# A decoder layer on one core: the first cross-attention is prepared in the last steps of self-attention, and the down projection's weights are split later

## What is computed

```python
x = x + attn(layernorm(x))          # 16 heads of 128, q and k RMS-normalised, no mask
x = x + xattn(layernorm(x), ctx)    # 16 heads of 32, causal mask, keys and values from ctx (361 x 128)
x = x + ffn(layernorm(x))           # silu(gate) * up, 1408 wide, then down; two of 8 experts
                                    # add low-rank terms of rank 16 to gate, up and down
```

## Time and profile before

| | |
|---|---|
| median of 3 runs | 2619.14 us (2618.99 to 2619.47) |
| the profiled execution | 2618.98 us, its span 2617.2 us |
| PE busy | 2477.4 us, 95% |
| DVE, ACT, POOL busy | 1545.2, 1343.3, 866.8 us |
| chain that ended last | PE 82%, DVE 7%, ACT 4%, issue 3% |
| granted clock of PE, mean | 0.979 |

### The profile page before, as it was taken

How to read it: one execution, slowest core, us unless ns; L and a number is a source line. 1 busy time by engine, 2 the same in 40 slices (tenths; PEclk the granted TensorE clock), 3 DMA queues, 4 the chain that set the end, 5 groups by cost and what they waited for, 6 DMA issues and landing times.

```text
span 2617.2 us, 47837 instructions
## 1 busy us (share of the span) xinstructions
PE 2477.4 (95%) x16390; PEld 1334.0 (51%) x16390; DVE 1545.2 (59%) x3589; ACT 1343.3 (51%) x4098; POOL 866.8 (33%) x801
## 2 busy tenths in 40 slices
PE   6999999999999999999769999999999999999998
PEld 3455455555554555445344464464464465465466
DVE  7777756666666666667355555554645645645634
ACT  4555555555555555555354454454554554454433
POOL 3333333333333333324123323323323322423412
PEclk9999999999999999999869999999999999999999
DMA  5677777776777668797320001001001001000000
GB/s 154 156 176 167 155 159 153 172 170 145 157 171 157 155 154 186 168 187 166 107 77 10 16 2 37 16 2 37 15 4 37 7 12 37 1 17 24 7 17 8
DMA packets 455401, 235.37 MB, mean 90 GB/s; under 512 B 389096, under 2 KB 391784, under 8 KB 455144
## 3 DMA queue, kind: packets, MB, share of 16 engines
q1 hardware_dynamic: 455144, 232.08, 38.3%
HBM read 78.66 MB, written 32.77 MB: 43 GB/s over the span
## 4 chain that ended last, share of the span: by engine, by line
PE 82%; DVE 7%; ACT 4%; issue 3%; POOL 1%; DMA 1%; SPq 1%; DVEq 0%; POOLq 0%; ACTq 0%
PE ps L1380 22%; PE ps L1381 21%; PE ps L1382 21%; PE ps L1513 3%; PE ps L1514 2%; PE ps L1515 2%; ACT mem L887 2%; PE ps L1624 2%; PE ps L1523 1%; PE ps L1527 1%; PE ps L1525 1%; PE ps L1566 1%; PE ps L1612 1%; PE ps L1586 1%; PE ps L1554 1%
## 5 line engine op out<-in xcount | busy, mean ns | idle before, releaser
L1380 PE MATMUL ps<-mem 128*128 128x512 f16 (+6 forms) x3924 | 1204.4, 326 | 59.5 <-issue 24.6
L1381 PE MATMUL ps<-mem 128*128 128x512 f16 (+6 forms) x3924 | 1217.5, 325 | 0.0
L1382 PE MATMUL ps<-mem 128*128 128x512 f16 (+6 forms) x3924 | 1201.1, 325 | 0.0
L1380 PEld LDWEIGHTS ps<-mem 128*128 128x128 f16 (+3 forms) x3924 | 407.6, 104 | 380.8 <-issue 75.8
L1382 PEld LDWEIGHTS ps<-mem 128*128 128x128 f16 (+3 forms) x3924 | 408.7, 104 | 311.7 <-issue 9.3
L1381 PEld LDWEIGHTS ps<-mem 128*128 128x128 f16 (+3 forms) x3924 | 410.4, 105 | 300.3 <-issue 9.6
L699 POOL TENSOR_TENSOR mem<-mem 128x500 f32<-128x500 f32 (+1 forms) x231 | 268.1, 1160 | 360.2 <-ACT mem L949 207.5
L649 POOL TENSOR_TENSOR mem<-mem 128x8 f32<-128x8 f32 x100 | 163.7, 1637 | 518.3 <-DVE mem L1021 518.3
L795 ACT ACTIVATE mem<-ps,mem 100x100 f32<-100x100 f32 x512 | 169.2, 345 | 223.4 <-DVE mem L1051 222.3
L1336 DVE TENSOR_TENSOR mem<-mem 128x500 f16<-128x500 f32 (+1 forms) x231 | 144.5, 649 | 188.7 <-ACT mem L931 184.7
L661 POOL TENSOR_TENSOR mem<-mem 100x400 f16<-100x400 f32 x128 | 158.4, 1237 | 175.7 <-ACT mem L805 175.7
(11 more groups left out here) (121 smaller groups left out, 3132.5 us busy)
## 6 DMA issues: line engine op xcount, KB each, us to landing
x<-mem SPq DMA_DIRECT2D x100, 256.0 KB, 2.9
mem<-x SPq DMA_DIRECT2D x75, 256.0 KB, 3.5
mem<-in_x SPq DMA_DIRECT2D x50, 256.0 KB, 3.6
mem<-x SPq DMA_DIRECT2D x12, 1000.0 KB
mem<-mem SPq DMA_DIRECT2D x32, 200.0 KB
out<-mem SPq DMA_DIRECT2D x6, 1000.0 KB
mem<-in_wq SPq DMA_DIRECT2D x16, 256.0 KB, 4.0
mem<-in_wk SPq DMA_DIRECT2D x16, 256.0 KB, 4.2
```

What stands on the lines that cost most here:

```text
L1380: pe.matmul(out_ap, ah, bh, start=(i == 0), stop=False)
L1381: pe.matmul(out_ap, ah, bl, start=False, stop=False)
L1382: mm = pe.matmul(out_ap, al, bh, start=False, stop=(i == len(pairs) - 1))
```

## The change

The preparation of the first cross-attention is taken out of `cross_attention` and put into the last four steps of self-attention by a function `begin_cross(n)` on PE, ACT and DVE:

- step 126 (`B_KEYS`): row tiles 0 and 1 are turned, keys 0 to 2;
- step 127 (`B_TURN`): key 3, row tiles 2 and 3;
- step 128 (`B_VALUES`): five value products;
- step 129 (`B_QUERIES`): four query products.

On PE this stands in a step ahead of the mix and the output projection; on ACT and DVE it is the last of a step. The wait for the last add (`s["add"], ALL`) in front of the first turn is gone. So that this is free of overlaps in memory, `yT` lies over weights that are used up, and qkT, vt and others move within the buffer.

The pieces of `bd` and `wd` are no longer among `B_PIECES` (16 are left). Piece 13, 14 and 15 are split in batches 0, 1 and 2 of the first cross-attention, one each. The others are loaded into the buffer `yn` once it is free, and are split in chunks 1, 3 and 5 of the feed-forward part of group 0 (`load_late`, `late_hi`, `late_lo`); the layer norm of the next group moves from chunks 6 and 7 to 8 and 9 there. For that, group 0 is written out, and the loop has four passes, groups 1 to 4. In the diff, the first `begin_cross` is DVE's, the second PE's; ACT's takes the same rows, values and queries as they come.

```diff
+        B_KEYS, B_TURN, B_VALUES, B_QUERIES = STEPS - 2, STEPS - 1, STEPS, STEPS + 1
...
         def over_groups(eng, group):
-            with eng.Fori(0, FULL - 1) as g:
+            group(0, GB, GB)
+            with eng.Fori(1, FULL - 1) as g:
                 group(g, GB, GB)
...
-        LN_STATS_CHUNK, LN_ROWS_CHUNK = FC - 5, FC - 4
+        def ln_chunks(g):
+            return (FC - 3, FC - 2) if isinstance(g, int) and g == 0 else (FC - 5, FC - 4)
...
-        add_pieces(bd_hi, bd_lo, bd, 1, E)
-        add_pieces(wd_hi, wd_lo, wd, FC, E)
-        assert len(B_PIECES) == 20
+        assert len(B_PIECES) == 16
+        LATE_AT = {1: 0, 3: 1, 5: 2}
+        late = yn.rearrange("p t e -> p (t e)")
...
         def beside_first(b):
-            return range(len(B_PIECES))[B_IN_A + 2 * b:B_IN_A + 2 * b + 2]
+            return range(len(B_PIECES))[B_IN_A + b:B_IN_A + b + 1]
...
                     sp.wait_ge(c["moved"], g + 1)
                     sp.wait_ge(c["yn"], g * 2 * NT + 2 * nt)
+                    if isinstance(g, int) and g == 0:
+                        for k in range(3):
+                            load_late(k)
+                        sp.wait_ge(c["latelo"], 3)
                     load_rows(yn, ahead, nxt, "yn_in")
...
+                def late_hi(k):
+                    act.wait_ge(c["late"], 16 * (k + 1 + (k == 2)))
+                    for hi, stage, _ in late_parts(k, True):
+                        op = act.activation(hi, stage, ACT.Copy, scale=W_SCALE)
+                    op.then_inc(c["latehi"], 1)
...
+            def begin_cross(n):
+                if n == B_KEYS:
+                    for t in range(2):
+                        row_lo(0, t, TM, t)
+                    for m in range(3):
+                        take_ck(0, GS, m)
+                if n == B_TURN:
+                    take_ck(0, GS, 3)
+                    for t in range(2, NT):
+                        row_lo(0, t, TM, t % 2)
...
+            def begin_cross(n):
+                if n == B_KEYS:
+                    pe.wait_ge(c["mask"], 5)
+                    pe.wait_ge(s["klo"], ALL)
+                    for t in range(2):
+                        turn_row(0, yn, t, TM, t)
+                    pe.wait_ge(c["wkv"], 16)
+                    pe.wait_ge(c["ctx"], 16)
+                    pe.wait_ge(s["vlo"], ALL)
+                    for m in range(3):
+                        keys(0, GS, m)
+                if n == B_TURN:
+                    pe.wait_ge(s["exp"], STEPS)
+                    keys(0, GS, 3)
+                    for t in range(2, NT):
+                        pe.wait_ge(c["lnlo"], t - 1)
+                        turn_row(0, yn, t, TM, t % 2)
+                if n == B_VALUES:
+                    for b in range(GB):
+                        cross_values(0, b)
+                if n == B_QUERIES:
+                    pe.wait_ge(c["lnlo"], NT)
+                    pe.wait_ge(c["wlo"], B_FIRST)
+                    for m in range(KC):
+                        queries(0, GS, m)
...
                 for u in projected_at(n):
                     project_qk(u)
+                begin_cross(n)
                 if 0 <= n - 1 < STEPS:
                     mix_values(n - 1)
                 for w in summed_at(n):
                     project_wo(w)
-            pe.wait_ge(s["add"], ALL)
-            pe.wait_ge(c["wlo"], B_FIRST)
-            pe.wait_ge(c["wkv"], 16)
-            pe.wait_ge(c["mask"], 5)
```

More of the change, by code:

```diff
@@ L277, in decoder_layer @@
                  "rl top rexp chain spread mT mTe a am ahi alo base gb sg0 ub lora gs us sgs "
-                 "h hhi hlo ad dt dsum dhi dlo yp add moved")
+                 "h hhi hlo ad dt dsum dhi dlo yp add moved late latehi latelo")
         c = {n: sem("c_" + n) for n in names.split()}
@@ L1330, in layer, with late_lo @@
                                       ALU.subtract).then_inc(c["alo"], 1)
+                def late_lo(k):
+                    dve.wait_ge(c["latehi"], k + 1)
+                    for lo, stage, hi in late_parts(k, False):
+                        op = dve.scalar_tensor_tensor(out=lo, in0=stage, scalar=W_SCALE, in1=hi,
+                                                      op0=ALU.mult, op1=ALU.subtract)
+                    op.then_inc(c["latelo"], 1)
                 def lo_h(i, j):
@@ L1500, in wide, with keys, cross_values @@
                                        yT_hi[:, e, 0:gs], yT_lo[:, e, 0:gs]) for e in range(KC)])
+            def keys(g, gs, m):
+                pe.matmul(ps[:, 2 + m, 0:gs], cwkv[:, m * P:(m + 1) * P], ctxT[:, 0:gs],
+                          start=True, stop=True).then_inc(c["ck"], 1)
+            def cross_values(g, b):
+                if b < 2:
+                    pe.wait_ge(c["cke"], g * KC + b + 1)
+                else:
+                    pe.wait_ge(c["ve"], g * GB + b - 1)
+                pe.matmul(ps[0:S, 2 + b % 2, :], ctxT[:, b * S:(b + 1) * S], cwkv[:, E:2 * E],
+                          start=True, stop=True).then_inc(c["v"], 1)
@@ new lines, in _ @@
+            for n in range(FIRST_STEP, STEPS + 2):
+                if 0 <= n + 1 < STEPS:
+                    scores(n + 1)
+                for u in valued_at(n):
+                    project_v(u)
+                for u in turned_tile(n):
+                    turn_rows(u)
+                for u in projected_at(n):
+                    project_qk(u)
+                begin_cross(n)
+                if 0 <= n - 1 < STEPS:
+                    mix_values(n - 1)
+                for w in summed_at(n):
+                    project_wo(w)
```

174 lines of the change are left out of this document (102 added, 72 removed).

## The result

The changed kernel takes 2602.83 us as the median of 5 runs (2597.96 to 2604.31), against 2619.47 of the kernel before in the same session (2618.99 to 2625.26). The ratio is 0.9929, interval 0.9917 to 0.994. It is worked out over all runs and is not the quotient of the two medians, which is 0.9936. On the 2619.14 of the prediction the ratio gives 2600.5, where 2605.2 was forecast and 2601.0 was the low end. The change gains more than I gave it. Built and timed again it gave 2604.27 against 2620.82, ratio 0.9934 (0.992 to 0.9947). One execution of the kernel with only group 0 unrolled took 6607 us, in a slow state, and stands in none of the figures.

What follows compares the result with a forecast made beforehand. PE bounds the feed-forward part; the self-attention tail and first cross-attention hold waits. Gains 6.7 + 5.9 + 0 + 1.2 = 13.8 us, taken from 2618.98, give 2605.2 us, range 2601 to 2611.5.

Steps and rivals of the forecast that it cites:

- part 4: Loop over groups: with group 0 outside, one of four DVE issue stalls goes, gaining 1.2 us (bounds 0 to 2.5).
- Part 1: Self-attention steps 126 to 129: cross-attention preparation fills PE idle time, first mask at about 1288.2 against 1294.88, gaining 6.7 us.
- rival D: Steps 127 and 128: two gaps keep the clock low through the moved work, slower at 2625.6 us; chance 0.04.
- C: Step 127: DVE's queue gives the filled gap back, mask stays at 1294.9, price 6.7 us, total 2611.9; chance 0.06.
- Part 2: First cross-attention: five weight pieces leave for later or go one per batch, gaining 5.9 us.
- rival A: First cross-attention: split gain comes only by half through low-clock scores or late DMA, 3 us less, 2608 to 2611; chance 0.12.
- Part 3: Feed-forward part of group 0: three late weight pieces are hidden in ACT and DVE idle time, costing 0 us.
- B: Feed-forward of group 0: late pieces not hidden, PE waits up to 2.3 us in three chunks, 2612 us; chance 0.08.

## Why the prediction fell short

The forecast was 13.8 us less. The two ratios give 18.6 and 17.3, the medians 16.6 in both sessions, the first profiles 16.3. Three steps of the sum failed. It took everything ahead of step 127 as unchanged and gave it no width in the range; the first profiles differ by 2.97 there. It took the rest of group 0 at 0; group 0 lost 2.45. It took part 4 at 1.2; the unrolling brought 2.55 to 2.9. For the first of these no reason was given; for the second it was that PE has no idle time there, which says nothing of its clock.

**Part 1, the preparation: right.** 6.7 was worked out, 6.5 came in the first pair of profiles, and the preparation alone gives 6.6; against the mean of the four old tails it is 7.2. The step through step 127 was right in detail: a wait of about 3 and one of about 2 (3.16 and 2.01), and the mix, forecast at 1263.1, at 1259.85; with 2.97 added for the earlier start of the step that is 1262.8. The clock was 1.00 from 1268 to 1288, so rival D was out, and the mask came early, so C was.

**Part 2, one piece per batch: right, a little small.** The mixes of the five batches stand 14.35, 23.99, 33.79, 43.01 and 54.94 us behind the mask; before they stood 15.84, 26.24, 39.29, 49.18 and 61.37. So the batches gained 1.49, 0.76, 3.25, 0.67 and 0.26, where the prediction had 1.3, then 4.1 for two, and 0.5. The gain of the split did not come by half (rival A), and the DMA came in time: the load is issued at 1286.69, and ACT begins the piece straight behind its exponentials:

```profile
1292.87 1.48 ACT L795 ACTIVATE mem<-mem 128x1408 f16<-128x1408 f32 x1
```

**Part 3, late pieces in group 0: the mechanism right, the figure for the group wrong.** The late pieces cost 0 as predicted, and B is out. The failed step is that the rest of group 0 was taken to be as it was ("PE has no idle time there"). The group took 2.45 more, because in these profiles the clock is low for longer at its router (+1.55) and again in the next cross-attention (+1.26). I had looked for the clock's answer in the tail alone, though the earlier trace rows show 0.66 in the very stretch whose rhythm the change alters. What makes it low at 137 us behind the router, with PE busy 5.90 of 6 us there and no edit near, no run settles; that one kernel of seven escapes both, with the same program up to there as another that does not, says that the edit alone does not decide it.

**Part 4, group 0 outside the loop: too small.** 1.2 was the stall in one pass. The kernel with this alone gained 2.9 in groups 0 to 4, and groups 1 to 4 of the kernel after 2.55. The term was mis-sized in its basis: it counted PE's wait behind one stall, which came as 0.9 (router to spread in group 1, 7.50 before and 6.59 after). Group 0, written out, also takes 0.25 less in the chunks, and with nothing but the unrolling 0.36 less between mask and router; the three stalls that are left are 2.28 to 2.40 instead of 2.51 to 2.54, and router to spread is 0.14 to 0.26 shorter behind them. Another 0.8 of the 2.55 is the clock's again: in group 2 spread to chunk 1 took 19.10 before, with 0.72 in the 6 us from 8 us behind the router, and takes 18.29 after, at 1.00. My upper bound of 2.5 was a little below what came.

**The sum and the range.** Terms 3 and 4 nearly cancel in the profile after (+2.45 and -2.55, where 0 and -1.2 stood). What made the profiled time 16.3 shorter instead of 13.8 is the start-up and self-attention before step 127, -2.97, for which I had nothing, neither in the sum nor in the range, and by which two executions of one kernel differ. The ratios put the kernels 17.3 and 18.6 us apart (0.9934 and 0.9929), the medians 16.6 in both sessions, and the stages from step 127 on give 13.3 between the first two profiles and 16.5 between the second pair (1371.18 and 1354.72), 14.9 in the mean; part of what the first pair lacks is the old tail, short in that profile. The 1.7 to 3.7 us that remain are not placed by any one profile; by the sum of the stages they would lie before step 127. In the eight other kernels the same remainder, the ratio's gain less that of the stages from step 127 on (against the mean of the two profiles of before), lies between -3.0 and +4.7, so it is of the size of the scatter. Whether the other layout of the buffer makes self-attention shorter on average stays open: it took 1206.7 in the mean of the three profiles with the old layout and 1205.6 in that of the nine with the new one, a difference far inside the scatter. That the time fell below the low end is thus in part luck, and what failed is also the range: its low end had the bounds of the terms, and neither the scatter of the stages ahead of the change nor that of the old tail.

## What to carry over

Work moved into waits of the bounding engine pays what it fills less the waits that it makes, and that can be worked out from the queue of the engine that takes the results; the largest thing left was the weight piece and the key copies standing in that queue ahead of what PE needed, and moving them took another 7.7 us from the tail. After a change of rhythm in a stretch with a low clock, expect the times at low clock to move and to be worth one to three us elsewhere, check the stages downstream even though no instruction of theirs changed, and take a second profile before a cause is given: here two executions of the same code differed by 2.3 and by 3.0 us in neighbouring stages. Before a range is drawn, know how far the long stages that are not touched differ between executions: here 3 us in each pair and 8.6 over twelve.

## What the runs showed of the hardware

- The granted clock of a stretch is not a property of the work in it. Group 0 took 200.3 to 200.4 us in six of the seven profiles with one piece per batch of the first cross-attention, 197.3 in the seventh, and 197.3 to 198.3 in the five with another distribution. The difference is 0.64 instead of 0.84 behind the router, and 0.72 instead of 1.00 in 6 us that begin 137 us later, where PE was busy 5.90 of them. The same program up to there gave 200.31 in one execution and 197.33 in another.
- A loop pass that follows a jump costs 1.4 us more than the same pass written out (198.91 against 197.53, 198.76 against 197.31). Of that, 0.7 to 1.0 stands near the start of the pass, where DVE shows 2.3 to 2.4 us of "issue" some tiny instructions in. The first pass, with no jump before it and no stall, still costs 0.9 more (198.43 against 197.52).
- A POOL product that reads SBUF and a DVE operation with two SBUF inputs hold each other back: DVE's low half took 1.21 instead of 0.68 us when the product had started first, and the product 1.54 instead of 1.25 when it started 0.43 us before the end of the low half.
- Some 1205 us of self-attention, with about 197 of the kernel's 235 MB of transfers in it (163 GB/s over 1207 us), took 1201.99 to 1210.62 us in twelve profiles. The stages behind the tail, with few transfers, repeated to 0.9 us in the two profiles of before and to 0.2 in those of the kernel after.
